# Copied columns in a GNN edge stage: every third group instead of every fourth, two columns to a VectorE operation

## What is computed

```python
edge_index = jnp.stack([src, dst])
h = jnp.maximum(_layernorm(x, axis=-1), 0.0)
x = x + L0(h, edge_index, edge_attr_128)
h = jnp.maximum(_layernorm(x, axis=-1), 0.0)
x = x + L1(h, edge_index)
# in L0:
msg_in = jnp.concatenate([x[src], x[dst], edge_attr], axis=-1)
h = jax.nn.relu(msg_in @ msg_W1 + msg_b1)
messages = h @ msg_W2 + msg_b2
aggregated = jax.ops.segment_sum(messages, dst, num_segments=x.shape[0])
```

## Time and profile before

| | |
|---|---|
| median of 3 runs | 3847.66 us (3846.76 to 3848.25) |
| profiled execution, its span from first to last instruction | 3844.1 us, 3.5 us under that median |
| busy: PE, VectorE (DVE), ScalarE (ACT), POOL | 2932.3, 2991.9, 2702.5, 2862.8 us |
| mean granted clock of TensorE | 0.880 of full speed |
| gathers in the first edge stage, in the second | 1469, 1518 |

### The profile page before, as it was taken

One profiled execution on the slowest core, in us unless ns is written; L12 is line 12 of the kernel. 1 busy time (PEld: TensorE's weight loads), 2 busy tenths in 40 slices (PEclk: granted clock), 3 DMA queues, 4 the chain that ended last, 5 costly groups with the idle time before them and its releaser, 6 DMA issues.

```text
span 3844.1 us, 84917 instructions
## 1 busy us (share of the span) xinstructions
PE 2932.3 (76%) x19349; PEld 2486.1 (65%) x19349; DVE 2991.9 (78%) x18185; ACT 2702.5 (70%) x13876; POOL 2862.8 (74%) x3038
## 2 busy tenths in 40 slices
PE   6788888888888888888767677767666767766776
PEld 5777788788777877787645555555555555555554
DVE  5677777777777777777568888888888888888887
ACT  4666666666666666666467777777777777777775
POOL 6777777777777777777677777777777777777775
PEclk8887877877888788878789999999999999999999
DMA  7455555555555555555343333333333333333332
GB/s 198 136 144 140 144 140 146 141 144 140 142 141 146 144 141 141 144 144 141 90 125 89 89 89 89 87 89 89 90 89 90 89 90 89 89 87 89 90 90 57
DMA packets 359405, 445.23 MB, mean 116 GB/s; under 512 B 169093, under 2 KB 215523, under 8 KB 358895
## 3 DMA queue, kind: packets, MB, share of 16 engines
q1 hardware_dynamic: 262911, 243.79, 21.7%
q0 software_dynamic: 95584, 195.75, 21.1%
q10 hardware_dynamic: 400, 0.20, 0.0%
HBM read 416.16 MB, written 23.28 MB: 114 GB/s over the span
## 4 chain that ended last, share of the span: by engine, by line
POOL 64%; issue 21%; PE 6%; DMA 4%; DVE 2%; ACT 2%; SPq 0%; DVEq 0%; ACTq 0%; POOLq 0%
POOL t_ring L1009 36%; POOL m_ring L997 28%; DMA m_ring<-tab_a,src_t 3%; PE bank L1669 2%; PE bank L1645 1%; PE bank L1656 1%; DVE m_pre L1752 1%; DMA tab_a<-m_pre 0%; DVE lone L958 0%; PE bank L1674 0%; ACT m_hid L1700 0%; ACT lone L1712 0%; DMA tab_x<-X 0%; SPq L2177 0%; DMA X<-in_x_dram 0%
## 5 line engine op out<-in xcount | busy, mean ns | idle before, releaser
L1009 POOL DMA_INDIRECT t_ring<-tab_l,src_t x1518 | 1440.4, 949 | 480.5 <-issue 462.0
L997 POOL DMA_INDIRECT m_ring<-tab_a,src_t x1469 | 1398.1, 952 | 459.5 <-issue 444.8
L1669 PE MATMUL bank<-w,m_attr_t 128*128 128x128 f32 x3128 | 702.0, 352 | 6.1 <-ACT m_attr_t L1709 5.2
L1712 ACT ACTIVATE lone<-HT 128x4 uint8 x6080 | 621.3, 190 | 69.5 <-issue 55.3
L1645 PE MATMUL bank<-m_hot,m_hid 128*128 128x32 f32 x3128 | 481.8, 302 | 229.4 <-ACT m_hid L1700 226.6
L1669 PEld LDWEIGHTS bank<-w,m_attr_t 128*128 128x128 f32 x3128 | 607.3, 241 | 47.4 <-DVE m_hot L1737 11.3
L1645 PEld LDWEIGHTS bank<-m_hot,m_hid 128*128 128x128 f32 x3128 | 450.9, 221 | 283.8 <-ACT m_hid L1700 275.9
L1752 DVE TENSOR_TENSOR m_pre<-bank,m_ring 128x512 f32<-128x512 f32 (+1 forms) x391 | 255.6, 654 | 411.8 <-DMA m_ring<-tab_a,src_t 328.0
L2434 PE MATMUL bank<-t_hot_t,t_win 96*128 96x512 bf16 x391 | 149.5, 382 | 556.1 <-DMA t_ring<-tab_l,src_t 489.6
L1700 ACT ACTIVATE m_hid<-m_pre 128x512 f32<-128x512 f32 x391 | 246.1, 629 | 426.7 <-DVE m_pre L1752 377.7
L958 DVE COPY lone<-HT 128x4 uint8 x6080 | 494.8, 195 | 62.6 <-issue 60.1
(11 more groups left out here) (267 smaller groups left out, 6110.1 us busy)
## 6 DMA issues: line engine op xcount, KB each, us to landing
m_ring<-in_edge_attr_dram SPq DMA_DIRECT2D x390, 256.0 KB
t_rows<-dst_rows SPq DMA_DIRECT2D x196, 256.0 KB
m_rows<-dst_rows SPq DMA_DIRECT2D x196, 192.0 KB
t_ring<-tab_l,src_t POOLq DMA_INDIRECT x1518
m_ring<-tab_a,src_t POOLq DMA_INDIRECT x1469
m_win<-tab_b SPq DMA_DIRECT2D x391, 24.0 KB
t_win<-tab_r SPq DMA_DIRECT2D x391, 24.0 KB
tab_b<-n_b SPq DMA_DIRECT2D x47, 96.0 KB
```

The source lines that it names most:

```text
L997: pool.indirect_dma_start(out=r.got[u][0:rows, j, :], out_offset=None, in_=k.tab_a, in_offset=bass.IndirectOffsetOnAxis(ap=k.src_t[0:rows, ...
L1009: pool.indirect_dma_start(out=r.got[u][0:rows, j, :], out_offset=None, in_=k.tab_l, in_offset=bass.IndirectOffsetOnAxis(ap=k.src_t[0:rows, ...
L1669: pe.matmul(p_hid[q % 2][:, e], lhsT=attr_t[q % 2][:, e], rhs=k.w1[:, 2, :], start=True, stop=False)
L1712: lambda out, col: act.activation(out, col, ACT.Copy), s["m_picked_s"])
```

## The change

V becomes 3: picked is each group g with g % 3 == 2, from 8 to 389, 128 groups, and their 128 columns are spread over three slots as 43, 43 and 42. VectorE takes 28, 28 and 26 of them, ScalarE 15, 15 and 16 (as before, by byte address, 4 bytes to a copy).

VectorE no longer copies. One TENSOR_SCALAR writes two columns: over the constant pair (all ones, 0) it does AND with column a and then XOR with column b, both read as per-partition scalar operands whose addresses come from registers. That leaves a XOR b and b. One TENSOR_TENSOR over the slot's columns then restores every a with one more XOR (L1015 of the changed kernel). The registers hold node numbers from `ids`, so each pair has register arithmetic ahead of it: two multiplications by 4 and two additions of HT's address. The loads are of 28, 28 and 26 registers on VectorE, from words 0, 43 and 86, and of 15, 15 and 16 on ScalarE, from words 28, 71 and 112; both are issued at the end of the slot before, VectorE's ahead of its tile work. SP waits for VectorE's picks before it fetches into an `ids` buffer again.

```diff
-V = 4
-PICKED = P // V
-BY_VECTOR = 16
+V = 3
+PICKS = (43, 43, 42)
+BY_VECTOR = (28, 28, 26)
...
+FIRST = -(-(U + 1 - V) // V)
...
-def pick_columns(nc, eng, k, m, g, first, many, move, done):
+def pick_load(nc, eng, k, m, g, by_vector):
...
+    first = sum(PICKS[:i]) + (0 if by_vector else BY_VECTOR[i])
+    many = BY_VECTOR[i] if by_vector else PICKS[i] - BY_VECTOR[i]
...
+def pair_load(nc, dve, k, m, g):
...
+    first, many = sum(PICKS[:i]), BY_VECTOR[i]
+    _, rows = nc.values_load_multi_w_load_instructions(
+        k.ids[n % 2][:, first:first + many], engines=[dve.engine], min_val=0, max_val=k.N - 1,
...
+def pair_move(dve, k, m, loaded):
...
+    words = k.HT[:].bitcast(U32)
+    for q in range(0, len(rows), 2):
+        last = dve.tensor_scalar(k.lone[:, n % 2, first + q:first + q + 2].bitcast(U32), k.first_only[:],
+                                 words[:, bass.ds(rows[q], 1)], words[:, bass.ds(rows[q + 1], 1)],
+                                 ALU.bitwise_and, ALU.bitwise_xor)
+    last.then_inc(m["m_paired"], 1)
+
+
+def pair_part(dve, k, m, g, loaded):
...
+    twos = k.lone[:, n % 2, first:first + len(rows)].bitcast(U32).rearrange("p (c a) -> p c a", a=2)
+    dve.wait_ge(m["m_paired"], (n - FIRST) * V + (g + SOONER) % V + 1)
+    dve.tensor_tensor(twos[:, :, 0], twos[:, :, 0], twos[:, :, 1], ALU.bitwise_xor).then_inc(m["m_picked_v"], 1)
...
 def fetch_picked(sp, k, m, src, n):
...
+    after(sp, m["m_picked_v"], (n - 2 - FIRST + 1) * V)
...
 def fast_vector(dve):
...
-                        pick_columns(nc, dve, k, s, g, 0, BY_VECTOR, dve.tensor_copy, s["m_picked_v"])
+                        pair_move(dve, k, s, loaded.get(g))
                     if at := before(rnd, u, 1, tail):
...
+                        if not tail:
+                            pair_part(dve, k, s, g + 1, loaded.get(g + 1))
                         hold(dve, s["m_hp"], g + 1)
...
+                    if not tail and g_now + 1 < k.groups:
+                        loaded[g_now + 1] = pair_load(nc, dve, k, s, g_now + 1)
                     dve_tile(dve, *slot(rnd, u))
```

More of the change, by code:

```diff
@@ L18 @@
 U8 = mybir.dt.uint8
+U32 = mybir.dt.uint32
 ALU = mybir.AluOpType
@@ L191, in gnn_program @@
         k.w1 = sb("w1", [P, 3, P], F32)
+        k.first_only = sb("first_only", [P, 2], U32)
         k.lone = sb("lone", [P, 2, P], F32)
@@ L956, in pick_columns, with pick_move @@
         skip_runtime_bounds_check_because="src names rows of the node features, as the gathers take it")
-    for q in range(many):
+    return n, first, places
+def pick_move(k, loaded, move, done):
+    if loaded is None:
+        return
+    n, first, places = loaded
+    for q, place in enumerate(places):
         last = move(k.lone[:, n % 2, first + q:first + q + 1].bitcast(U8),
-                    k.HT[:].bitcast(U8)[:, bass.ds(places[q] - k.ht_at, 4)])
+                    k.HT[:].bitcast(U8)[:, bass.ds(place - k.ht_at, 4)])
     last.then_inc(done, 1)
+def pair_load(nc, dve, k, m, g):
+    n, i = (g + SOONER) // V, (g + SOONER) % V
+    if not picked(k, n * V + V - 1):
+        return None
+    if i == 0:
+        if n == FIRST:
+            dve.wait_ge(k.s_ht, k.n_ht)
+        dve.wait_ge(m["m_ids"], 16 * (n - FIRST + 1))
+        after(dve, m["m_hp"], (n - 1) * V if n - 2 >= FIRST else 0)
+    first, many = sum(PICKS[:i]), BY_VECTOR[i]
+    _, rows = nc.values_load_multi_w_load_instructions(
+        k.ids[n % 2][:, first:first + many], engines=[dve.engine], min_val=0, max_val=k.N - 1,
+        skip_runtime_bounds_check_because="src names rows of the node features, as the gathers take it")
+    return n, first, rows
+def pair_move(dve, k, m, loaded):
+    if loaded is None:
+        return
+    n, first, rows = loaded
+    words = k.HT[:].bitcast(U32)
[5 more added lines that the diff above has]
+def pair_part(dve, k, m, g, loaded):
+    if loaded is None:
+        return
+    n, first, rows = loaded
+    twos = k.lone[:, n % 2, first:first + len(rows)].bitcast(U32).rearrange("p (c a) -> p c a", a=2)
+    dve.wait_ge(m["m_paired"], (n - FIRST) * V + (g + SOONER) % V + 1)
+    dve.tensor_tensor(twos[:, :, 0], twos[:, :, 0], twos[:, :, 1], ALU.bitwise_xor).then_inc(m["m_picked_v"], 1)
 def fetch_picked(sp, k, m, src, n):
@@ L1584, in body @@
                     sp.wait_ge(k.s_wtc, 1)
-                    fetch_picked(sp, k, s, t["src"], U // V)
+                    for n in range(FIRST, (U + 1) // V + 1):
+                        fetch_picked(sp, k, s, t["src"], n)
                     return
@@ L1705, in body @@
                     act_tile(act, *slot(rnd, u))
+                    g = rnd * U + u
                     if not tail:
-                        g = rnd * U + u
                         after(act, s["m_attrp"], g + 1)
                         act.activation(attr_t[u % 2][:], p_attr[u % 2][:], ACT.Copy).then_inc(s["m_attr"], 1)
-                        placed(nc, act, k, s, g)
-                        pick_columns(nc, act, k, s, g, BY_VECTOR, PICKED - BY_VECTOR,
-                                     lambda out, col: act.activation(out, col, ACT.Copy), s["m_picked_s"])
+                        placed(act, k, s, g)
+                        pick_move(k, loaded.get(g), lambda out, col: act.activation(out, col, ACT.Copy), s["m_picked_s"])
                     act_sources(act, *slot(rnd, u))
                     rows(rnd, u, tail)
+                    if not tail and g + 1 < k.groups:
+                        loaded[g + 1] = pick_load(nc, act, k, s, g + 1, False)
+            loaded = {}
             rounds(act, k.groups, body, 2)
```

40 lines of the change are left out of this document (21 added, 19 removed).

## The result

The changed kernel takes 5680.27 us (median; 5676.88 to 5682.09), the kernel before 3847.43: a ratio of 1.476, 95% interval 1.474 to 1.478. The forecast was 4980 us with a range of 3920 to 5250. It had the sign and the two kinds of register load; the time lies above its range.

A forecast was written before the change was run, and what follows sets the result against it. POOL's gathers were taken to set the pace, VectorE having slack. After the change VectorE's queue needs 4.65 + 3.0 = 7.65 us a group instead of 4.706, over 384 groups +1130 us: 4980 us, range 3920 to 5250.

The forecast's parts named there:

- the sign: Whole kernel: the change makes it slower, +1130 us; the slow side together had 0.80.
- the two kinds of register load: VectorE's queue: register loads would last near 2 us or near 6 us.
- VectorE's loads: First term, VectorE's queue: loads from words 0, 43, 86 take 1.9, 6.2, 5.8 us, mean 4.65.
- A pair: VectorE's datapath: one two-column operation with two per-partition operands takes 0.194 us, both operands paid in full.
- the faster rival: VectorE: loads go by size, second operand hides; 33 fewer gathers are the whole effect, 3806 to 3835 us; chance 0.15.
- Loads go by size: VectorE's loads: 2.0 us wherever they begin, the datapath decides, 3940 to 3980 us; chance 0.16.
- one penalty per load: VectorE's loads: 1.2 us extra on two of three, mean 2.8 us, total 4075 to 4306 us; chance 0.12.
- no change: Whole kernel: time stays between the faster rival's and that of loads by size; chance 0.05.
- every register by itself: VectorE's loads: each register paid singly, first load too, mean 6.1 us, total 5530 us; chance 0.02.
- the second term of the sum: VectorE's queue, from a load's end to the next load's start: tile work, masks and ten pairs, 3.0 us.
- edits at nothing: ScalarE's copies and loads, SP's wait ahead of its fetch, the wait on paired columns: all put at no cost.
- ten pairs: VectorE's datapath: the next load starts with eight instructions still to run, so only ten pairs, 1.94 us, precede it.

The follow-up runs named there:

- the table: Kernel before plus 34 extra register loads each on VectorE and ScalarE, of 1 to 32 registers from various words, load durations tabulated; 3860.3 us in all.
- the kernel with copies: Changed kernel with single copies for pairs, split 48, 40, 40 (32, 24, 24 to VectorE): 4113.4 us; without SP's wait 3889.7.
- the version with 20 copies: Changed kernel with single copies, no SP wait, split 44, 44, 40, with 20, 20, 20 columns to VectorE: 3816.1 us, ratio 0.9922.

## Why the prediction was wrong

**Its terms, one by one.** VectorE's loads: 4.65 us in the mean, measured (1.86 + 6.26 + 5.80)/3 = 4.64, with some luck: the forecast had 0.56 us for the first register and 0.21 for each further one, the table has 0.31 for one register, and from there to the change's 28 it is 0.22 each, and the two errors cancel. A pair 0.194, measured 0.191: the second pointer operand is paid in full, so the faster rival was out (its 1.89 us for pairs at 0.13 should read 1.87, which moves nothing). Register arithmetic 0.06, measured 0.069. Gathers 1436, as said. POOL waits for VectorE, as said. "Loads go by size", "one penalty per load" and "no change" are out by the loads alone. The time is nearest to that of "every register by itself", 5530, and that one is out too, by the first load's 1.86 us.

**The step that failed** is the second term of the sum, the rest of a slot: "I take 3.0." It measured 4.9, and two of the "edits at nothing" are what it lacks. The first: "The wait on the paired columns has L1747's 0.28 us in front of it." That the wait is short is beside the point. The queue stands in it until the last pair has ended, so it can't run eight instructions ahead, and the load behind it starts with three instructions left on the datapath. Averaged over the 335 slots of the trace from 400 to 3600 us, 4.90 us pass from the end of a load to the start of the next: 1.23 to the first pair (forecast: 1.2 of tile work and masks), then not ten pairs (1.94) but all of them, 2.47 from the first start to the last, 0.28 until the last ends, and 0.92 until the load starts. In half of the slots that last part is 0.35 at most, and the rest of its mean is waits in some of them. 2.47, 0.28 and 0.35 are 1.16 more than ten pairs. Moving the load ahead of the wait saved 1.15.

The second: "SP now waits ... four groups behind SP", where I named the next edge rows as what is queued behind. What mattered was the store of the finished node tile, behind the same wait, which ScalarE needs at once, and PE and VectorE through ScalarE. VectorE's 137.7 us of waits for PE are 0.41 us a group; without SP's wait the time fell by 0.39 a group, and by 0.58 in the kernel with copies, whose slots are shorter.

**The sum.** Forecast +1130 us, measured +1833. Of the 703 missing, 442 are the wait on the paired columns and 149 SP's wait, each by the run that takes it away. About 112 are left, 0.3 us a group. 0.14 of these are my rounding of 3.14 to 3.0; the rest no run here separates. The trace has 0.57 us a group of waits ahead of the load, of which the run without SP's wait gave back 0.39.

**Where the mechanism was right with a wrong rule.** The forecast took a multiple of eight words as the condition, which the trace before could not tell from four. For VectorE's start words, 43 and 86, the two say the same, so the number came out right, and that is luck. ScalarE's start words tell them apart in the changed kernel itself. The forecast had 3.1 us for its loads of 15 registers from word 71 and from word 28 alike; the first of these rows is from word 71, the second from word 28, a multiple of four:

```profile
L959 ACTq TENSOR_LOAD <-gen_win_id x1: 3241/3241/3241, 1866.3 to 1866.3; - x1
...
L959 ACTq TENSOR_LOAD <-gen_base x1: 1432/1432/1432, 1885.1 to 1885.1; - x1
```

The Trainium skill ("Runtime: NRT & Kernel Launch", Instruction fetch mechanics) has about 200 ns a register, in bulk too. The table has 226 ns each for 16 registers from word 1 and 69 each for 16 from word 4: the page's figure is near for the one kind of load only.

**The whole loss**, by the runs: loads off a multiple of four words 1129 us, the load behind the wait 442, SP's wait 149, and pairs in place of copies 362 in the kernel where that can be seen alone. They overlap and don't add up. What the change was after, 33 gathers less, is 41 us by POOL's pace; of it the version with 20 copies keeps 29 (3845.5 to 3816.1), and gathers of 960 ns instead of 952 are the size of the rest.

## What to carry to other kernels

Start a multi-register load at a multiple of four words (16 bytes) and load a multiple of four: 28 registers then take 1.86 us, and from word 43 6.26. A wait of an engine on its own last instruction costs little by itself, but it takes away the cover of whatever blocks the queue behind it; look at what that is before calling the wait free. And when a wait is put into a queue that carries several duties, as SP's here, go through everything behind it: the first thing that is late need not be the one that belongs to the change.

## What I had not expected of the hardware

A register load's cost has steps of four: 5, 6 and 7 registers take 602, 826 and 1056 ns, 8 take 597. A copy of one 4-byte column has a pitch of 0.071 us on VectorE, an operation on two columns with two operands from register addresses 0.191, so the two-in-one form lost 0.05 us a pair before its other costs. And 196 us hung on where a load of 1.6 us stands among the same instructions: behind a few long ones 1.36 us of it are covered, behind many short ones 0.90.
